# Transposing the attention probabilities in halves of 64 rows, and grouping the value products, in a fused attention and expert kernel

## The reference

```python
q = l2norm(x @ Wq.T per head) * q_scale      # 8 batches, 16 heads, 512 tokens, head width 64
k = l2norm(x @ Wk.T per head) * k_scale
v = x @ Wv.T per head
attn = softmax(einsum('bhid,bhjd->bhij', q, k) * 64 ** -0.5)
out = einsum('bhij,bhjd->bhid', attn, v)
```

## Time and profile before

| | us |
|---|---|
| median of 3 runs | 1490.31 (1489.26 to 1490.5) |
| the profiled execution's own time | 1490.81 |
| its span in the profile | 1489.0 |
| TensorE matmuls busy in the span | 1364.8 (92%) |
| VectorE busy | 1097.5 (74%) |
| ScalarE busy | 1063.9 (71%) |
| GpSimd busy | 644.8 (43%) |

### The profile page before, as it was taken

One profiled execution on the slowest core, in us unless ns is written; L12 is line 12 of the kernel. 1 busy time (PEld: TensorE's weight loads), 2 busy tenths in 40 slices (PEclk: granted clock), 3 DMA queues, 4 the chain that ended last, 5 costly groups with the idle time before them and its releaser, 6 DMA issues. The chain is left out here.

```text
span 1489.0 us, 27979 instructions
## 1 busy us (share of the span) xinstructions
PE 1364.8 (92%) x7626; PEld 872.4 (59%) x7626; DVE 1097.5 (74%) x2179; ACT 1063.9 (71%) x2650; POOL 644.8 (43%) x1279
## 2 busy tenths in 40 slices
PE   4899999999999999999999999999999367799997
PEld 4555565556655555665566556655554345577775
DVE  4578768776876776688768776876775698588887
ACT  3678777776876787688767776876776456577776
POOL 2344435433444454344335433534442756344443
PEclk8899999999999999999999999999999689899999
DMA  5000000000000000000000000000000200433331
GB/s 124 2 1 2 1 1 2 1 4 1 1 2 3 2 1 4 2 1 2 3 1 2 1 4 1 2 2 1 1 2 17 55 1 0 110 90 88 98 89 41
DMA packets 53192, 28.40 MB, mean 19 GB/s; under 512 B 8720, under 2 KB 51224, under 8 KB 53016
## 3 DMA queue, kind: packets, MB, share of 16 engines
q1 hardware_dynamic: 51832, 25.99, 7.0%
q10 hardware_dynamic: 1184, 0.40, 0.1%
HBM read 24.16 MB, written 2.23 MB: 18 GB/s over the span
## 5 line engine op out<-in xcount | busy, mean ns | idle before, releaser
L794 DVE TENSOR_REDUCE neg_max<-bank 128x1 f32<-128x512 f32 x512 | 346.8, 685 | 179.9 <-PE bank L503 164.4
L667 ACT ACTIVATE probs<-bank,neg_max 128x512 f32<-128x512 f32 x512 | 352.2, 688 | 143.6 <-DVE neg_max L794 141.6
L515 PEld LDWEIGHTS bank<-ident,probs 128*128 128x128 f32 x2048 | 224.7, 141 | 257.7 <-issue 184.6
L515 PE MATMUL bank<-ident,probs 128*128 128x128 f32 x2048 | 328.6, 284 | 1.4 <-ACT probsT L675 1.3
L537 PE MATMUL bank<-probsT,v_tok 128*64 128x512 f32 x1024 | 275.7, 617 | 0.8 <-DVE probsT L801 0.8
L503 PE MATMUL bank<-operands 64*128 64x512 f32 x1536 | 248.9, 429 | 10.0 <-ACT probs L667 8.4
L49 POOL TENSOR_TENSOR rn_t<-rn 128x16 f32<-128x16 f32 x192 | 42.8, 223 | 399.7 <-DVE rn L40 389.7
L642 ACT ACTIVATE qk_tok<-bank 128x256 f32<-128x256 f32 x256 | 97.6, 381 | 114.4 <-PE bank L475 114.0
L801 DVE COPY probsT<-bank 128x512 f32<-128x512 f32 x256 | 173.7, 679 | 0.5 <-PE bank L515 0.4
L503 PEld LDWEIGHTS bank<-operands 64*128 64x128 f32 x1536 | 125.6, 186 | 67.3 <-ACT probs L667 27.3
L675 ACT ACTIVATE probsT<-bank 128x512 f32<-128x512 f32 x256 | 153.0, 598 | 13.3 <-PE bank L515 0.7
(11 more groups left out here) (212 smaller groups left out, 2427.2 us busy)
## 6 DMA issues: line engine op xcount, KB each, us to landing
probsT<-gate_scratch SPq DMA_DIRECT2D x64, 256.0 KB, 4.8
out<-x_all SPq DMA_DIRECT2D x8, 256.0 KB, 2.3
probsT<-in_L_ffn_fc_w SPq DMA_DIRECT2D x1, 1024.0 KB, 9.6
raw<-in_L_attn_Wq SPq DMA_DIRECT2D x1, 512.0 KB, 4.8
raw<-in_L_attn_Wk SPq DMA_DIRECT2D x1, 512.0 KB, 7.5
raw<-in_L_attn_Wv SPq DMA_DIRECT2D x1, 512.0 KB, 8.7
raw_o<-in_L_attn_Wo SPq DMA_DIRECT2D x1, 512.0 KB, 8.6
probsT<-in_L_ffn_sh_w SPq DMA_DIRECT2D x2, 256.0 KB, 2.7
```

The costliest lines, as they stand in the source:

```text
L515: last = nc.tensor.transpose(T_BANK[i % 2][:, j * P:(j + 1) * P], probs[:, i % 4, j * P:(j + 1) * P], ident[:])
L667: nc.scalar.activation(probs[:, i % 4], s_bank(hp, i)[:], ACT.Exp, bias=neg_max[:, i:i + 1], accum_out=row_sum[:, hp % 2, i:i + 1]).then_i ...
L794: nc.vector.reduce_max(neg_max[:, i:i + 1], s_bank(hp, i)[:], AX.X, negate=True).then_inc(max_done, 1)
```

## The change

Transposes now go by pairs of tiles. For each pair there are sixteen transposes of 64 rows by 128 columns instead of eight of 128 by 128; the lower and the upper 64 query rows alternate and go to two banks: half 0 of both heads to `T_BANK[0]`, half 1 to `T_BANK[1]`. ScalarE copies the first bank and VectorE the second, one copy each a pair (four each a slot, as before). A pair's transposes wait for both tiles' exponentials and for both copies of the pair before. In TensorE's queue they stand directly behind the scores of the next pair: pair 3 of the slot before at step 0, pairs 0, 1 and 2 at steps 2, 4 and 6. The value products come two key tiles at a time, at steps 4 and 6. The copies stand behind the exponentials (ScalarE) and the row maximum (VectorE) of steps 1, 3, 5 and 7; at step 1 it is the copy of pair 3 of the slot before.

```diff
-            P_LAG = 3
+            def half_tiles(hp, pair, half):
+                at = pair * P + half * DH
+                return probsT[:, hp % 2, :, :, at:at + DH]
...
-                    def transpose_probs(u, i):
-                        pe.wait_ge(p_done, S_TILES * u + i + 1)
-                        semaphore, count = {0: (t_dve, -1), 1: (t_dve, 0), 2: (t_dve, 1), 7: (t_dve, 2)}.get(i, (t_act, i - 2))
-                        after(pe, semaphore, 4 * u + count)
-                        for j in range(NT):
-                            last = nc.tensor.transpose(T_BANK[i % 2][:, j * P:(j + 1) * P],
-                                                       probs[:, i % 4, j * P:(j + 1) * P], ident[:])
-                        last.then_inc(t_ready, 1)
+                    def transpose_probs(u, pair):
+                        pe.wait_ge(p_done, S_TILES * u + 2 * pair + 2)
+                        after(pe, t_act, 4 * u + pair)
+                        after(pe, t_dve, 4 * u + pair)
+                        pe.nop(nofuse=True)
+                        for head in range(2):
+                            for j in range(NT):
+                                for half in range(2):
+                                    rows = slice(half * DH, (half + 1) * DH)
+                                    at = (NT * head + j) * DH
+                                    last = nc.tensor.transpose(T_BANK[half][:, at:at + DH],
+                                                               probs[rows, (2 * pair + head) % 4, j * P:(j + 1) * P],
+                                                               ident[rows, rows])
+                                    if (head, j) == (1, NT - 1):
+                                        last.then_inc(t_ready, 1)
...
-                            if tail and i >= S_TILES - NT:
-                                weigh_values(u - 1, hp - 1, i - (S_TILES - NT))
-                            if tail and i < P_LAG:
-                                transpose_probs(u - 1, S_TILES - P_LAG + i)
-                            if main and i >= P_LAG:
-                                transpose_probs(u, i - P_LAG)
+                            if tail and i == 0:
+                                transpose_probs(u - 1, NT - 1)
+                            if main and i in (2, 4, 6):
+                                transpose_probs(u, i // 2 - 1)
+                            if tail and i in (4, 6):
+                                weigh_values(u - 1, hp - 1, i - 4)
+                                weigh_values(u - 1, hp - 1, i - 3)
...
-                        after(act, t_ready, g - 3)
+                        after(act, t_ready, S_TILES * u + 2 * (i // 2) - 2)
...
-                    def copy_transposed(u, hp, i):
-                        act.wait_ge(t_ready, S_TILES * u + i + 1)
-                        if i == 1:
+                    def copy_transposed(u, hp, pair):
+                        act.wait_ge(t_ready, S_TILES * u + 2 * pair + 1)
+                        if pair == 0:
                             after(act, av_done, u - 1)
...
+                        nc.scalar.activation(half_tiles(hp, pair, 0), T_BANK[0][:].rearrange("p (h j q) -> p h j q", h=2, j=NT),
                                              ACT.Copy).then_inc(t_act, 1)
...
-                            if main and i > P_LAG:
-                                copy_transposed(u, hp, i - P_LAG)
+                            if tail and i == 1:
+                                copy_transposed(u - 1, hp - 1, NT - 1)
+                            if main and i in (3, 5, 7):
+                                copy_transposed(u, hp, i // 2 - 1)
```

More of the change, by code:

```diff
@@ L668, in exponentials @@
                                              accum_out=row_sum[:, hp % 2, i:i + 1]).then_inc(p_done, 1)
-                    def copy_transposed(u, hp, i):
-                        act.wait_ge(t_ready, S_TILES * u + i + 1)
-                        if i == 1:
+                    def copy_transposed(u, hp, pair):
+                        act.wait_ge(t_ready, S_TILES * u + 2 * pair + 1)
+                        if pair == 0:
                             after(act, av_done, u - 1)
-                        t, head = i // 2, i % 2
-                        nc.scalar.activation(probsT[:, hp % 2, head, :, t * P:(t + 1) * P],
-                                             T_BANK[i % 2][:].rearrange("p (j q) -> p j q", j=NT),
+                        nc.scalar.activation(half_tiles(hp, pair, 0), T_BANK[0][:].rearrange("p (h j q) -> p h j q", h=2, j=NT),
                                              ACT.Copy).then_inc(t_act, 1)
@@ L794, in row_max, with copy_transposed @@
                         nc.vector.reduce_max(neg_max[:, i:i + 1], s_bank(hp, i)[:], AX.X, negate=True).then_inc(max_done, 1)
-                    def copy_transposed(u, hp, i):
-                        dve.wait_ge(t_ready, S_TILES * u + i + 1)
-                        if i == 0:
+                    def copy_transposed(u, hp, pair):
+                        dve.wait_ge(t_ready, S_TILES * u + 2 * pair + 2)
+                        if pair == 0:
                             after(dve, av_done, u - 1)
-                        t, head = i // 2, i % 2
-                        nc.vector.tensor_copy(probsT[:, hp % 2, head, :, t * P:(t + 1) * P],
-                                              T_BANK[i % 2][:].rearrange("p (j q) -> p j q", j=NT)).then_inc(t_dve, 1)
+                        nc.vector.tensor_copy(half_tiles(hp, pair, 1),
+                                              T_BANK[1][:].rearrange("p (h j q) -> p h j q", h=2, j=NT)).then_inc(t_dve, 1)
                     def invert_sums(u, hp):
@@ L860, in slot @@
                                 row_max(u, hp, i)
-                            if tail and i < P_LAG:
-                                copy_transposed(u - 1, hp - 1, S_TILES - P_LAG + i)
+                            if tail and i == 1:
+                                copy_transposed(u - 1, hp - 1, NT - 1)
                             if tail and i == 1:
                                 invert_sums(u - 1, hp - 1)
-                            if main and i == P_LAG:
-                                copy_transposed(u, hp, 0)
+                            if main and i in (3, 5, 7):
+                                copy_transposed(u, hp, i // 2 - 1)
                             if front_b and i == QT_AT + 1:
```

## The result

| | before | after |
|---|---|---|
| median of the runs side by side | 1490.0 (1489.3 to 1490.5) | 1616.0 (1613.3 to 1617.4) |
| ratio to before | | 1.084, 95% interval 1.0825 to 1.0863 |
| span in the profile | 1489.0 | 1615.7 |

The forecast was 1620, the measured time 1616. That agreement is partly an accident: one price was too high, and losses that I had left at nothing or in a rival took the place of the difference.

What follows compares the result with a forecast made beforehand. TensorE was taken to set the pace. Its own work made 16.59 us a slot, new waits 18.61 against 16.38: +138 over 62 slots, less 9 for filled gaps, 1490.8 + 129 = 1620 us; range 1580 to 1735.

Steps and rivals of the forecast that it cites:

- Which waits would come at steps 0 to 5: TensorE's transposes at steps 2 and 4 wait 0.96 us for ScalarE's copy; a projections' gap of 0.8 stays empty.
- the projections: Steps 0 to 3: from one projection to the next 1.44 us, the second waiting for ScalarE's copy of v.
- grouped values: Steps 4 and 6: value products of two steps together take 1.86 us, one change of shape saved.
- the forecast's slot: Attention stage: one slot grows from 16.38 to 18.61 us, new waits included.
- the halves' price: TensorE's transposes: a pair of 64-row halves costs 0.11 us, so a pair of tiles costs what it did.
- the bound that I had named for moving columns as the pace: Transposes at 0.055 us a pair of halves: 1512 us; chance 0.03 for a pace between 0.044 and 0.10.
- The argument from weight loads: Transposes: two 64-row loads in the scores cost 0.11 us, like one of 128 rows, so halving rows buys no speed.
- 0.3 before they are due: Step 0: ScalarE's copy of pair 2 ends 0.3 us before pair 3's transposes need it, so no wait.
- The 9 us that the forecast took back: Gap behind projection 0: router's 0.80 us and y's transposes, 0.44, fall into it in 7 batches, -9 us.
- VectorE's extras: Steps 5 to 7: VectorE's extra work may cost a few us, counted as nothing and left to the range.
- the rival with 0.22: New TensorE gaps drop the granted clock to 1.2 GHz, up to 1.7 us lost each: 1673 to 1725 us; chance 0.22.
- The forecast called itself wrong: TensorE's timeline: wrong if steps 2 and 4 lack the idle, half pairs aren't 0.11 apart, or clock leaves 1.00 mid-stage.

Runs made afterwards that it cites:

- without VectorE's collision: The kernel after, with VectorE making the high part of the weighted values from the PSUM bank instead of by a CAST from SBUF: 1602.8 us, ratio 1.076.
- the order kernel: The kernel after, with transposes behind the projection at steps 0 and 2 and behind the value products at steps 4 and 6: 1512.6 us, ratio 1.015.
- The fastest kernel: the order kernel, with VectorE making the high part of the weighted values from the PSUM bank instead of by a CAST: 1455.6 us, ratio 0.977.

## Why the prediction came out

**Right.** Which waits would come at steps 0 to 5, where, and nearly their sizes: 0.86 and 0.82 us for 0.96, the projections 1.43 for 1.44, grouped values 1.87 for 1.86. Whole tiles in the new order gave the forecast's slot to 0.02 us. That the two queue orders make the waits is shown by moving each alone: ScalarE's copy gave back 68 us, TensorE's transposes 111. The two overlap, since together they would be more than the 126 lost.

**The step that failed: the halves' price.** "I take 0.11 a pair: the pair of tiles costs what it did." Sixteen halves take 0.64 with a change of shape and 0.52 up to scores of the same 64-row shape (549.82 to 550.34): about 0.061 a pair, near the bound that I had named for moving columns as the pace (0.055). The argument from weight loads was the wrong reading: it took 0.11, the pace of the scores' load pairs, for a limit. The scores stream 512 columns a matmul, so their loads may have had no need to be faster; no run varies that. By the rule that the prediction quoted beside it (the Trainium skill, TensorE: Matmul & The Clock Gate, LDWEIGHTS) one load of 128 columns takes 0.107 us. Here two of them, on different groups of rows, went through every 0.061. The measurement decides. With 0.061 the forecast's slot is 18.61 less 4 x 8 x 0.049, 17.04, and the kernel 1620 less 97, 1523. (Its own sum has a slip too small to matter: 0.90 + 0.93 + 0.10 - 0.15 is 1.78, not 1.77.)

**What took its place.** The clean slots of a batch sum to 139.7 before and 154.2 after, +14.5:
- Slot 6, without extras, is 17.61 and not 17.04. The largest part is at step 0. The prediction has ScalarE's copy of pair 2 end "0.3 before they are due"; it turned into a wait of 0.28 (scores to transposes is 1.09 at 617.29, and 0.81 at 614.03, where nothing waits). Once the halves are fast, the transposes are due earlier. Against 16.39 the slot is +1.22, in 8 slots 9.8 of the 14.5.
- The turn of the loop, +2.2 (idle time 2.9 for 0.7, means of five): nothing of this was forecast.
- The slots with extras have the last 2.5. The first quarters of slots 2, 4 and 5 are 5.65, 5.38 and 5.46, against 4.33 in slot 6, and they are the same without VectorE's collision. In each, ScalarE has an activation of 0.78 us for an extra at the slot's start, ahead of the last exponential and the copy of pair 2, and the transposes of step 0 wait 1.30, 1.18 and 1.26 for that copy. In slot 5, ScalarE and then TensorE:
```profile
598.83 0.78 ACT L696 ACTIVATE m_out<-bank,mod 128x512 f32<-128x512 f32 x1 [0.78 <-PE bank L576]
...
600.17 0.59 ACT L685 ACTIVATE probsT<-bank 128x512 f32<-128x512 f32 x1
```
```profile
600.87 0.71 PE L523 MATMUL bank<-ident,probs 64*128 64x64 f32 x16 [1.26 <-ACT probsT L685]
```
The 9 us that the forecast took back for the router logits and the transposes of y came as forecast (behind them the second projection waits 0.20 us or not at all, for 0.64), but this wait in the same slots is larger. VectorE's extras, left "at nothing", no run isolates.

In 7.75 batches the 12.3 without the turn are 95 us, and five turns 11: 106 of the 126. The clock takes most of the other 20. It is the rival with 0.22, which came in part. Two neighbouring stretches of after, columns as in the earlier trace rows:
```profile
622.63:626.03 3.40, 1.95 (x22) 1.59 (x22) 2.76 (x5) 2.41 (x8) 0.02 (x1) 0.98 0.00 0
626.03:629.43 3.40, 3.40 (x26) 2.38 (x27) 0.88 (x2) 3.00 (x9) 0.00 (x0) 0.52 0.01 2
```
As in the earlier trace rows, a stretch with gaps is followed by one at 1.2 GHz. But a fall cost mostly 0.5 to 0.8 us (slots with one against the same slots without: 18.1 for 17.61, 19.1 for 18.65, 19.2 for 18.41), not 1.7; I take it that much of what runs slower stands ahead of a wait. Right behind the turn, where the clock can stay low for 6.8 us, it cost 1.2 to 1.7 (18.7 to 19.1 for 17.4). And it came in two slots of five: of the 48 slots of batches 1 to 6, 19 had one, together some 15 us by this estimate. The forecast called itself wrong if pairs of halves were not 0.11 apart, or if the clock left 1.00 in mid-stage; by both it was, though its time came true.

**The collision** is another loss that I hadn't looked for, worth 13 us in after and 57 in the order kernel, though the kernel before has it too (mean 0.75 us, against 0.43 undisturbed). The Trainium skill (SBUF — State Buffer, SBUF: two separate sides) says that VectorE and GpSimd share a pair of ports, which one instruction holds for its whole length; on VectorE's side this goes for instructions in a mode that uses both ports, or with two inputs in SBUF. The trace agrees: 0.43 alone, up to 2.12 beside a 1.9 us multiply, and no spread (0.68 to 0.69) for the form that reads PSUM. The prediction wrote that no GpSimd work is moved. Its order is not, but the change moves it in time against VectorE's.

## What to carry to other kernels

Before grouping instructions by shape, ask what each one was filling: here grouping the value products gained 24 us, and moving the transposes out of the projections' gap lost 111. Where an in-order engine must wait for a copy, put work that needs nothing between the wait's start and the instruction that waits; in slot 6 the same transposes cost two idle times directly behind the scores and none one group later. Price a new form by the stage that limits it: a pace read where something else is the limit is a bound, not a price. And sum all slots of a batch, not the plain one alone: here the slots with extras and the turn of the loop took back a good part of what slot 6 gained.

## What the runs showed of the hardware

- Two fp32 transposes of 64 rows and 128 columns, on the two halves of the rows, take 0.061 us together, where one of 128 rows takes 0.11.
- At the same 842 us of busy TensorE in 1020 us the granted clock fell 21 times in after and never in its twin with whole tiles; in the order kernel and its twin it fell 14 times and 3. The fastest kernel has its five falls all at the turns of the loop, behind idle times of 3.0 to 3.5 us. Why the others come is not shown.
- A CAST of 128x512 from SBUF on VectorE is stretched from 0.43 to 2.1 us by GpSimd's multiply; a multiply with one operand in PSUM is not.
- TensorE idles at the turn of a loop: 0.4 to 1.0 us before, 1.1 to 1.8 in the twin of the fastest kernel with whole tiles, 3.0 to 3.5 in the fastest, which has halves.
